# The ahead chain's products joined to 256 columns, and one group of tokens instead of four ahead of the scan

## The reference

```python
def step(params, kvt):                       # 1024 steps, each over 2 tokens
    g = jax.grad(loss_fn)(params, k_t, v_t)  # mean((silu(k @ W1 + b1) @ W2 + b2 - v) ** 2)
    new_params = tuple((p - LR * gp for p, gp in zip(params, g)))
    return (new_params, None)
params, _ = jax.lax.scan(step, (W1, b1, W2, b2), (k, v))
return _mlp(params, x @ W_Q)
...
x = x + 0.5 * ffn(_layernorm(x))    # 8 experts, the best 2 of each token, and a shared one
x = x + attn(_layernorm(x))         # the scan above, k and v from x @ W_KV
x = x + 0.5 * ffn(_layernorm(x))
```

## Time and profile before

| | |
|---|---|
| median of 3 runs | 511.83 us (509.27 to 514.12) |
| the profiled execution's own time | 513.47 us |
| its span, first to last instruction | 511.6 us |
| first mixture of experts | 0 to about 147 us |
| way in, up to the first sums of the scan | 147 to 192.4 us |
| 15 turns with both chains, 9.54 to 9.79 us each | 192.4 to about 336 us |
| way out, second mixture of experts | the rest |
| PE busy | 441.3 us, 86% of the span |

### The profile page before, as it was taken

How to read it: one execution, slowest core, us unless ns; L and a number is a source line. 1 busy time by engine, 2 the same in 40 slices (tenths; PEclk the granted TensorE clock), 3 DMA queues, 4 the chain that set the end, 5 groups by cost and what they waited for, 6 DMA issues and landing times.

```text
span 511.6 us, 10071 instructions
## 1 busy us (share of the span) xinstructions
PE 441.3 (86%) x2962; PEld 363.6 (71%) x2962; DVE 277.3 (54%) x1045; ACT 245.3 (48%) x650; POOL 233.8 (46%) x335
## 2 busy tenths in 40 slices
PE   7896787999935999999999999999986869999950
PEld 5342477999932578999999999974532468999940
DVE  4852334555528556666666666655871443555524
ACT  2872134555530355556556556535871324555520
POOL 4176575444530033545545545551066665544430
PEclk9999999999975999999999999999998799999985
DMA  8961316101036500000000000000011316101019
GB/s 232 282 221 42 94 49 182 36 27 31 10 91 173 131 1 1 1 1 3 2 1 2 1 3 1 1 1 2 2 37 47 100 43 188 33 27 31 24 35 228
DMA packets 34515, 30.91 MB, mean 60 GB/s; under 512 B 3838, under 2 KB 30085, under 8 KB 34464
## 3 DMA queue, kind: packets, MB, share of 16 engines
q1 hardware_dynamic: 24608, 19.17, 13.7%
q0 software_dynamic: 4544, 8.47, 5.2%
q10 hardware_dynamic: 5312, 2.62, 1.9%
HBM read 15.55 MB, written 15.61 MB: 61 GB/s over the span
## 4 chain that ended last, share of the span: by engine, by line
PE 75%; DVE 9%; issue 5%; DMA 4%; another core or an unknown queue 3%; ACT 2%; POOL 1%; ACTq 1%; DVEq 0%; POOLq 0%
PE bank L1220 20%; PE bank L701 15%; PE bank L688 14%; PE bank L659 4%; PE bank L559 3%; DMA stage<-y_dram 3%; PE bank L649 3%; PE bank L1043 2%; PE bank L676 2%; PE bank L1108 2%; PE bank L1076 2%; PE bank L1081 2%; DVE stats L409 1%; PE bank L1102 1%
## 5 line engine op out<-in xcount | busy, mean ns | idle before, releaser
L1600 DVE TENSOR_TENSOR sq<-bank,relu 128x512 f32<-128x512 f32 x86 | 59.4, 691 | 106.5 <-ACT relu L801 73.6
L1350 POOL DMA_INDIRECT y_dram<-y_out,stage x78 | 76.4, 980 | 71.3 <-ACT y_out L827 66.1
L701 PE MATMUL bank<-proj_w,sq 128*128 x624 | 88.1, 285 | 12.1 <-DVE sq L1600 7.3
L1345 POOL DMA_INDIRECT slots_dram<-rows,slots x64 | 63.3, 989 | 67.5 <-ACT rows L752 35.4
L701 PEld LDWEIGHTS bank<-proj_w,sq 128*128 128x128 f32 x624 | 77.0, 194 | 16.7 <-issue 14.8
L688 PE MATMUL bank<-tileT,tile_w 128*128 128x128 f32 x624 | 83.9, 279 | 2.9 <-ACT tileT L793 2.8
L801 ACT ACTIVATE relu<-bank 128x512 f32<-128x512 f32 x94 | 55.8, 595 | 53.3 <-PE bank L688 25.2
L688 PEld LDWEIGHTS bank<-tileT,tile_w 128*128 128x128 f32 x624 | 77.3, 195 | 3.4 <-ACT tileT L793 3.1
L827 ACT ACTIVATE y_out<-bank,stage 128x128 f32<-128x128 f32 x78 | 28.7, 367 | 48.2 <-PE bank L701 38.2
L1215 POOL TENSOR_TENSOR sq<-sq,last_rows 128x128 f32<-128x128 f32 x32 | 14.6, 456 | 50.1 <-DVE sq L1196 50.1
L559 PE MATMUL bank<-ones 128*128 128x512 f32 x38 | 22.1, 730 | 15.5 <-DVE res L1651 12.7
(11 more groups left out here) (269 smaller groups left out, 1061.6 us busy)
## 6 DMA issues: line engine op xcount, KB each, us to landing
slots_dram<-pad SPq DMA_DIRECT2D x2, 2535.0 KB, 13.9
stage<-slots_dram SPq DMA_DIRECT2D x18, 260.0 KB
fc_w<-experts SPq DMA_DIRECT2D x1, 2048.0 KB, 20.3
proj_w<-experts SPq DMA_DIRECT2D x1, 2048.0 KB
stage<-y_dram SPq DMA_DIRECT2D x8, 256.0 KB, 5.5
stage<-y_dram ACTq DMA_DIRECT2D x8, 256.0 KB, 6.1
y_dram<-y_out,stage POOLq DMA_INDIRECT x78, 2.6
res<-x SPq DMA_DIRECT2D x4, 256.0 KB, 4.2
```

The lines of the kernel that those rows point to most:

```text
L701: last = nc.tensor.matmul(bank[4 + i % 2][:, 0:P], sq[:, i % 2, f_cols], proj_w[:, k, f_cols], start=j == 0, stop=j == FJ - 1)
L1345: nc.gpsimd.indirect_dma_start(to, bass.IndirectOffsetOnAxis(slots[:, n:n + 1], 0), rows[:, k, b, :], None, bounds_check=limit, oob_is_err ...
L1350: nc.gpsimd.indirect_dma_start(y_dram.ap(), bass.IndirectOffsetOnAxis(tiles[:, t, P:P + 1].bitcast(U32), 0), y_out[:, t % YBUFS, :], None, ...
L1600: nc.vector.tensor_tensor(wide_of(i)[2], wide_of(i)[0][:], wide_of(i)[1], ALU.mult)\
```

## The change

Four things are done.

1. In `ahead` the products `a @ w2` and the transposing of `a` become one product of `a` with `[w2 | identity]`, 256 columns wide, into `t_bank`; one ACT copy (`act_guess_rows`) of 256 columns takes both results. The products `e @ e` and `e @ w2t` become one of `e` with `[e | w2t]`. The two products that open these sums are widened with zeros, since both halves of the bank are opened at once: `offset` with `[identity | 0]`, and `da_old` with `[0 | rows]`. The transposed `th` goes to `h_bank` instead of `t_bank`, and with the banks the waits move: `pe_first` waits for `u`, `pe_offset` for `erows`.
2. `pe_w1_sums` of `ahead` reads keys rounded to float32r (`k_rows_r`, four casts on POOL) and so becomes one pass instead of two.
3. The order within a turn is written anew on PE, ACT and DVE, and the order in which the parameters are updated with it: `final`'s first, then `ahead`'s.
4. The way in: only group 0 is added and normalised ahead of the scan's first steps; POOL adds the two ways of groups 1 to 3 together; DVE puts the rest of the adding, statistics and scaling of groups 1 to 3 between the operations of first steps 0 and 1, and ACT normalises their 12 blocks there. `kk` and the key rows get places of their own so that unread results aren't overwritten. `pe_keep_busy` shrinks from ten products to three. Slots of step 0 hold only group 0's parts 4 and 3, steps 1 and 2 hold groups 1 and 2, and group 3's five parts stand alone behind the steps.

```diff
-        rounded = sb("rounded", [P, 2, T], F32R)
+        rounded = sb("rounded", [P, 3, T], F32R)
         k_r = rounded[:, 0, :]
         kk_r = rounded[:, 1, :].rearrange("p (b d) -> p b d", d=P)
+        k_rows_r = rounded[:, 2, :].rearrange("p (b d) -> p b d", d=P)
...
-        k_rows = stage[:, 2 * T:3 * T].rearrange("p (b d) -> p b d", d=P)
-        kk = stage[:, 3 * T:4 * T].rearrange("p (b d) -> p b d", d=P)
+        k_rows = rows[:, 1, :, 0:P]
+        kk = sb("kk", [P, NBLK, P])
...
+        w2_ident = sb("w2_ident", [P, 3 * P], F32R)
+        ahead_w2, ident_r, ident_zero = w2_ident[:, 0:P], w2_ident[:, P:2 * P], w2_ident[:, P:3 * P]
+
+        e_w2t = sb("e_w2t", [P, 2 * P], F32R)
+        ahead_e, ahead_w2t = e_w2t[:, 0:P], e_w2t[:, P:2 * P]
+
+        guess_rows = sb("guess_rows", [P, 3 * P + 2], F32R)
+        ahead_guess, zero_rows, ahead_rows = guess_rows[:, 0:P], guess_rows[:, P:3 * P], guess_rows[:, 2 * P:3 * P + 2]
...
-            return slot % KEY_PARTS, 1 + slot // KEY_PARTS
+
+            if slot < KEY_PARTS:
+                return ((4, 0), (3, 0), (0, NG), (0, NG), (0, NG))[slot]
+            return slot % KEY_PARTS, slot // KEY_PARTS
...
+                if g == 0:
+                    nc.scalar.copy(k_r[:, cols], bank[5][:]).then_inc(kr_done, 1)
                 nc.scalar.copy(k_t[:, cols], bank[5][:]).then_inc(kcol_done, 1)
...
-            if part == 1:
+            if part == 1 and g:
                 pool.wait_ge(kcol_done, g + 1)
                 nc.gpsimd.tensor_copy(k_r[:, g * COLS:(g + 1) * COLS], k_t[:, g * COLS:(g + 1) * COLS])\
                   .then_inc(kr_done, 1)
+            elif part == 3:
+                pool.wait_ge(krows_copied, g + 1)
+                nc.gpsimd.tensor_copy(k_rows_r[:, g * GRP:(g + 1) * GRP, :], k_rows[:, g * GRP:(g + 1) * GRP, :])\
+                  .then_inc(krowsr_done, 1)
...
             x = step.chain
             pe.wait_ge(offset_done, 2 * step.block + (1 if x is ahead else 2))
-            if step.n:
-                pe.wait_ge(x.d_done, step.n)
-            wait_param(pe, step, turn, "b1_half" if x is ahead else "w1")
-            mm(x.d_bank, x.offset, ident_r[:], stop=False)
+            if x is ahead:
+                if step.n:
+                    pe.wait_ge(x.erows_done, step.n)
+                wait_param(pe, step, turn, "w2")
+                nc.tensor.matmul(x.t_bank[:, 0:2 * P], x.offset, ident_zero, start=True, stop=False)
+            else:
+                if step.n:
+                    pe.wait_ge(x.d_done, step.n)
+                wait_param(pe, step, turn, "w1")
+                mm(x.d_bank, x.offset, ident_r, stop=False)
...
-            mm(x.d_bank, old.chain.aa[:, old.to, :], old.chain.ed[:, old.to, 0, :], start=False, stop=False)
+            mm(x.t_bank if x is ahead else x.d_bank, old.chain.aa[:, old.to, :], old.chain.ed[:, old.to, 0, :],
+               start=False, stop=False)
...
+            if x is ahead:
+                nc.tensor.matmul(x.t_bank[:, 0:2 * P], x.a, w2_ident[:, 0:2 * P], start=False, stop=True)\
+                  .then_inc(x.yrows_done, 1)
+            else:
+                mm(x.d_bank, x.a, x.w2, start=False).then_inc(x.yrows_done, 1)
...
 
             x, old = step.chain, step.old
+            pe.wait_ge(old.chain.ee_done, old.m + 1)
+            if x is ahead:
+                pe.wait_ge(x.guess_done, step.n + 1)
+                pe.wait_ge(x.d_done, step.n)
+                nc.tensor.matmul(x.d_bank[:, 0:2 * P], x.ee[:, old.to, :], zero_rows, start=True, stop=False)
+                return
             pe.wait_ge(x.rows_done, step.n + 1)
...
-            mm(x.d_bank, x.e, x.w2t, start=step.old is None).then_inc(x.da_done, 1)
+            if x is ahead:
+                nc.tensor.matmul(x.d_bank[:, 0:2 * P], x.e, e_w2t[:], start=step.old is None, stop=True)\
+                  .then_inc(x.da_done, 1)
+            else:
+                mm(x.d_bank, x.e, x.w2t, start=False).then_inc(x.da_done, 1)
...
             pe.wait_ge(x.d_done, step.n + 1)
-            weights = mm(x.d_bank, k_rows[:, step.block, :], x.ed[:, step.to, 1, :].bitcast(F32))
-            if x is final:
-                weights.then_inc(done, 1)
+            if x is ahead:
+                pe.wait_ge(x.ee_done, step.m + 1)
+                mm(x.d_bank, k_rows_r[:, step.block, :], x.ed[:, step.to, 1, :])
+            else:
+                mm(x.d_bank, k_rows[:, step.block, :], x.ed[:, step.to, 1, :]).then_inc(done, 1)
...
+        def act_guess_rows(act, step):
+
+            x = step.chain
+            act.wait_ge(x.yrows_done, step.n + 1)
+            nc.scalar.copy(guess_rows[:, 0:3 * P].rearrange("p (a d) -> p a d", d=P)[:, 0::2, :],
+                           x.t_bank[:, 0:2 * P].rearrange("p (a d) -> p a d", d=P)).then_inc(x.guess_done, 1)
...
-            nc.vector.scalar_tensor_tensor(x.u, x.rows[:, 0:P].bitcast(F32), 1.0, x.t_bank[:, P:2 * P], ALU.subtract,
+            if x is ahead:
+                dve.wait_ge(x.guess_done, step.n + 1)
+                dve.wait_ge(x.t_done, step.n + 1)
+            else:
+                dve.wait_ge(x.rows_done, step.n + 1)
+            th_rows = (x.h_bank if x is ahead else x.t_bank)[:, P:2 * P]
...
+            da = x.d_bank[:, P:2 * P] if x is ahead else x.d_bank[:, 0:P]
+            nc.vector.scalar_tensor_tensor(x.ed[:, step.to, 1, :], x.slope, 1.0, da, ALU.subtract,
...
+            if x is ahead:
+                dve.wait_ge(x.da_done, step.n + 1)
+                ee = x.d_bank[:, 0:P]
+            else:
+                dve.wait_ge(x.ee_mm, step.m + 1)
+                ee = x.y_bank[:, 2 * P:3 * P]
+            nc.vector.tensor_tensor(x.ee[:, step.to, :], ee, mask, ALU.mult).then_inc(x.ee_done, 1)
...
-            pool_key_part(pool, 1, 0)
-            pool_key_part(pool, 4, 0)
+            for g in range(1, NG):
+                cols = slice(g * COLS, (g + 1) * COLS)
+                pool.wait_ge(y_in[g], 32)
+                nc.gpsimd.tensor_tensor(y_rows[:, 0, cols], y_rows[:, 0, cols], y_rows[:, 1, cols], ALU.add)\
+                  .then_inc(y_added, 1)
 
...
+                cols = slice(g * COLS, (g + 1) * COLS)
+                r = res[:].rearrange("p b d -> p (b d)")[:, cols]
+                if g == 0:
+                    dve.wait_ge(shared_added, NG)
+                    dve.wait_ge(y_in[0], 32)
+                    dve_link(dve, nc.vector.tensor_tensor(r, r, y_rows[:, 1, cols], ALU.add), at)
+                else:
+                    dve.wait_ge(y_added, g)
+                nc.vector.tensor_tensor(r, r, y_rows[:, 0, cols], ALU.add).then_inc(res_done, 1)
+                dve.wait_ge(res_done, g + 1)
+                norm_moments(dve, at, g, norm_stats(dve, at, g))
...
+                lo, hi = ((GRP, 2 * GRP), (2 * GRP, NBLK), (0, 0))[n]
+                if hi == 0:
+                    return
+                if slot == 0:
+                    rsqrt_guess(dve, at, lo, hi)
+                elif slot < 4:
+                    rsqrt_newton(dve, at, lo, hi)
+                    if slot == 3:
+                        norm_shift(lo, hi)
+                elif n == 0:
+                    add_group(dve, 2)
+                    add_group(dve, 3)
...
-            stats_there = add_routed(0, True)
-            for g in range(NG):
-                norm_moments(dve, at, g, stats_there)
-            normalise(dve, at)
+            add_group(dve, 0)
+            norm_scale(dve, at, 0, GRP)
+            for b in range(GRP):
+                nc.vector.tensor_scalar(ln[:, b, :], res[:, b, :], mv[:, b, 0:1], rs_y[:, b:b + 1],
+                                        ALU.subtract, ALU.mult).then_inc(ln_done, 1)
+            add_group(dve, 1)
             dve_key_part(dve, 2, 0)
-            dve_key_part(dve, 4, 0)
             dve.wait_ge(vcol_done, 1)
             for step in first_steps():
                 dve_key_part(dve, *key_part(5 * step.n))
+                dve_norm_part(dve, step.n, 0)
                 dve_aa(dve, step)
                 dve_key_part(dve, *key_part(5 * step.n + 1))
+                dve_norm_part(dve, step.n, 1)
                 dve_u(dve, step)
                 dve_e(dve, step, -1)
...
+                dve_norm_part(dve, step.n, 4)
+            for part in range(KEY_PARTS):
+                dve_key_part(dve, part, NG - 1)
             dve.wait_ge(vcol_done, NG)
...
-            pe.wait_ge(res_done, NG)
-            pe_keep_busy(5)
+            pe.wait_ge(res_done, 1)
+            pe_keep_busy(3)
             pe.wait_ge(params_in, 16 * 7)
             nc.tensor.transpose(bank[7][:, 0:P], wq_sb[:], ident[:]).then_inc(wqT_done, 1)
-            for part in NG_PARTS_FIRST:
+            for part in NG_PARTS_FIRST[0:3]:
                 pe_key_part(pe, part, 0)
```

239 lines of the change are left out of this document (117 added, 122 removed).

## The result

| | before | after |
|---|---|---|
| median | 511.75 us (509.27 to 514.47, 8 runs) | 516.74 us (514.44 to 521.02, 8 runs) |
| the profiled execution's own time, its span | 513.47, 511.6 us | 516.78, 514.8 us |
| way in, first addition to first sums | 38.9 us | 46.5 us |
| scan, first to last error of `final` | 146.3 us | 142.6 us |
| the rest (start, end, and the 4.4 us between sums and first error) | 326.4 us | 325.7 us |

The change makes the kernel 1% slower: ratio 1.0095, 95% interval 1.007 to 1.012. I had forecast 505.2 us. Both halves of the forecast were off: the turns give 3.7 us instead of 6.6, and the way in, forecast at no change, costs 7.6 us. The two profiled executions lie 3.3 us apart and the medians 5.0, since the profiled execution of before was itself 1.7 us above its median.

A forecast was written before the change was run, and what follows sets the result against it. PE (8.4 us a turn) was taken as the bound, final's chain (7.8) close behind; 513.47 - 6.6 (turns) + 0 (way in) = 506.9 us, a median of 505.2 us since that execution lay 1.6 us above its median; range 499 to 513 us.

The forecast's parts named there:

- Price of a pass, 0.1125 us: PE in the scan's turns: weight loads follow each other by 0.1125 us, so five passes less are 0.56 us a turn.
- 256 columns cost 0 more: The turn's seven widened passes: 0 us more each than a pass now, from ends of 0 and 0.10 us.
- The third rival: Scan: 256 columns at 0.84 ns each, seven passes 0.10 us dearer, turn 9.8 us, 515.9 us in all; chance 0.08.
- Waits of 1.2 us a turn: PE in the new turn: waits at nine places, together 1.2 us, on 7.88 us of passes, giving 9.1 us.
- the 6.6 us: Scan: 15 turns with both chains, each 0.44 us shorter, make 6.6 us less, between 0 and 11.
- My walk: New order followed with trace durations: turn 9.1 us; on the way in, first sums at 191.6 us.
- The chain of 7.8 us: Dependent operations of final through a turn: some 7.8 us by addition, close behind PE's 8.4.
- The first rival: Scan: final's chain with its queueing sets the turn, 9.45 us, 1.4 us less in all, 510.4 us; chance 0.22.
- Way in, 0: Way in, first addition to first sums: no net change, between -4 and +8 us.
- The clock, 0.8 us: Way in: 0.8 us allowed for PE's clock perhaps falling to the lower level for a part of it.
- The fourth rival: Way in: the clock falls in its steps and stays low to the scan, +6 us, 511.2 us; chance 0.12.
- up to 8: Way in: cost in us if PE's clock is low for two steps and the tail.

The follow-up runs named there:

- w1_one_pass: The kernel before, with only ahead's W1 sums reading keys rounded to float32r, one pass instead of two: turn 9.44 us, 512.46 us in its one run.
- four_extra_wide: The changed kernel with each 256-column offset product of ahead done three times in the turns, four more passes a turn: turn 9.44 us, one run.
- apart_pool_filled: apart_mended with POOL adding groups 2 and 3 behind group 0's scaled blocks, two unread products in step 1, one ahead of the first sums: 0.9927 of before.
- joined_old_order: The changed kernel with before's way in and before's turn order on PE, ACT and DVE's first half, dropped passes left out: turn 10.11 us, one run.
- normalise_apart: The changed kernel with DVE adding groups 2 and 3 right behind group 1, and ACT normalising one group per step behind its copy: 0.9965 of before.
- fillers: The changed kernel with six unread products instead of three ahead of group 0's keys, and two more in steps 1 and 2: 1.0022 of before.
- old_way_in_start: The changed kernel with before's way in, apart_mended's two edits and one unread product ahead of the first sums: 0.991 of before.
- apart_mended: normalise_apart with old_guess and yrows of early[1] moved into the wait for a, and sums waiting for one group's cast: 0.9977 of before.
- four_extra_passes: The changed kernel with each aa product of ahead done three times in the turns, four more 128-column passes a turn: turn 9.59 us, one run.

## Why the prediction was wrong

**Price of a pass, 0.1125 us: right.** `w1_one_pass` gives 0.12 a turn for the one pass that it saves.

**256 columns cost 0 more: right.** The next weight load follows L1062 after 0.12 us, `four_extra_wide` has 0.115 us from one such pass to the next, and an `offset` of 256 columns takes 0.38 us from an idle PE, as forecast. The third rival falls. The row is from the timeline of `apart_pool_filled`:

```profile
169.88 0.38 PE L1043 MATMUL bank<-w_ident,ahead_offset 128*128 128x256 f32 x1 [2.95 <-ACT ahead_offset L1192]
```

**Waits of 1.2 us a turn: too small, and with it the 6.6 us.** The waits measure 1.4 us (9.31 less 70 passes of 0.1125), so the turn is 9.31, not 9.10; 0.25 of 0.56 us arrive, 3.7 us in all. My walk had the waits for `a` and guess of `early[1]` at 0.2 each, as they are. It had none in front of `ahead`'s W1 sums, where PE waits 0.24 us in every turn, by the code for DVE's reading of `ee` from the bank that `da` and `ee` now share. I knew that the waits move with the banks, and priced only those that I met on the way; I should have gone through each product that opens a bank and asked who reads that bank last. `joined_old_order` shows how large waits can become, 0.55 us a turn against the kernel before, though not that the banks alone make them.

**The chain of 7.8 us: added up wrongly.** The first rival (the turn stays) rests on it. Its own terms give more: eight products at 0.52 are 4.16, the single pass 0.35, ACT 0.86 and 0.32, six of DVE 2.1 to 2.5, the passes in front 0.8, in all 8.6 to 9.0 us. That is above PE's 8.4. So I had no ground to call PE the bound with the chain close behind it, and 0.22 was too small a chance for the first rival, which was half right: the turn lies between its 9.45 and my 9.10. The experiments say the same, since added passes are swallowed in part, and moving one pass lengthens the turn by 0.22 us.

**Way in, 0: wrong, +7.6 us.** Its stations, forecast against measured: group 0 normalised 159.8 and 162.1 us, since I held POOL's additions for covered; "POOL has no other work there" was true and beside the point, DVE had. First product 163.9 and 166.7 us. `d` of step 0 168.8 and 173.4; then 8.4 and 8.6 us to the next two, measured 10.06 and 10.12. First sums 191.6 and 200.2. The places of the stacked work were right (adding groups 2 and 3 in front of `aa`, four and eight blocks in front of the silus): `normalise_apart` moves that work and gets 6.5 us back, a better clock included. The error is one of size: group 0 is late by some 2 us for POOL's additions, and each step behind it is 1.5 to 1.8 us longer than in my walk, in which PE's products run at the upper clock, with 0.8 us added for it at the end.

**The clock, 0.8 us: the term that failed most.** It fell in three stretches for 20.4 us, and the mean clocks of all executions say the same. The fourth rival, to which I gave 0.12, is what happened, at the same time as the stacked work and not instead of it. `fillers`, which only adds products that nobody reads, gets 3.7 us back, with half the low clock in its profiled execution, and so puts some 3.7 us on the clock. I had worked out "up to 8" for two steps and the tail, and had the row that showed the fall behind a half empty PE; I chose the low end because "it may fall for a part of the way". The Trainium skill ("TensorE: Matmul & The Clock Gate", Why this matters for your kernels) warns of idle gaps of PE between bursts. Here the longest single gap in the stretches ahead of the three falls was 2.35 us.

**The range.** 499 to 513 took rivals one at a time. The measured 516.7 is two of them together, too small a gain in the turns and the clock on the way in, both with the same sign: the turns give 2.9 us less than forecast and the way in costs 7.6 us more.

What stays open: how the 7.6 us divide exactly. Order and clock are not independent (in the one profiled execution of `normalise_apart` the low clock is 6.8 us shorter without a further product), so 6.5 and 3.7 us can't be added. How much of the new 0.24 us wait could be had back. And which part of `joined_old_order`'s 0.55 us is the banks', which part that of DVE's order.

## What to carry to other kernels

Joining products saves passes but can tie readers to a bank: before pricing the saved passes, list for each product that opens the bank who must have read it, and expect to rewrite the order. Work that used to stand ahead of a chain is not hidden by being put between its steps; put it behind the operation whose result another engine is still working on, not in front of the next dependent one. Where PE has long waits, price everything on it at both clock levels, and try one unread product in the wait right ahead of the stretch that matters. And add up a chain's terms twice before calling another engine the bound.

## What the runs showed of the hardware that I had not expected

- One addition of POOL (1.27 us) holds up a DVE TENSOR_TENSOR of 4 columns to 1.15 us instead of 0.16, and four TENSOR_SCALAR operations to 3.06 instead of 1.11 us beside two of them. Small operations that fell between the additions took their usual 0.16 us.
- A short wait can be followed by the lower clock, or not: `w1_one_pass`, with PE busy 1.24 of the 2.90 us ahead of the scan, had the lower level for the 3.4 us behind them, and lost 1.1 us there. In `old_way_in_start`, with an unread product of two passes in the wait (busy 3.17 of 3.40 us), the clock stayed up. `apart_mended` had the wait without the product, and it stayed up too.
- The clock changes between executions of the same instructions: after, `four_extra_passes` and `four_extra_wide` have the same way in, and were at the lower level for 20.4, 13.6 and 20.5 us (46.5, 45.4 and 46.5 us long).
